# First routed mixture: six sequences are sorted inside the linear attention ahead of it, and the chunks are six and two sequences

## The reference, cut to what matters

```python
def lightning_attn(q, k, v):            # 16 heads of 64, 4 key/value heads, chunks of 128 tokens
    def step(kv, (qi, ki, vi)):
        scores = einsum('bhtd,bhsd->bhts', qi, ki) * mask
        o = einsum('bhts,bhsd->bhtd', scores, vi) + einsum('bhtd,bhde->bhte', qi * q_dec, kv)
        kv = blk_dec * kv + einsum('bhtd,bhte->bhde', ki * k_dec, vi)
        return kv, o

def mixture(x, w_gate, w1, w3, w2):      # 8 experts, the best 2 of each token, hidden width 256
    top_logits, sel = top_k(x @ w_gate, 2)
    probs = softmax(top_logits)
    y[e] = (silu(x @ w1[e]) * (x @ w3[e])) @ w2[e]
    return sum over k of probs[k] * y[sel[k]]

x = x + lightning_attention(layernorm(x))        # "light"
x = x + mixture(layernorm(x))                    # "moe1", the first one
x = x + differential_attention(layernorm(x))     # "diff"
x = x + mixture(layernorm(x))                    # "moe1", the second one
```

## Time and profile before

| what | us |
|---|---|
| median of 3 runs | 2660.44 (2657.58 to 2661.44) |
| the profiled execution | 2654.68 |
| its span | 2652.8 |
| light, first to last matmul | 1162.8 to 1546.4 |
| first mixture, light's last add to its own last add | 1547.2 to 1841.5 |
| second mixture, first to last matmul | 2367.3 to 2631.9 |

### The profile page before, as it was taken

How to read it: one execution, slowest core, us unless ns; L and a number is a source line. 1 busy time by engine, 2 the same in 40 slices (tenths; PEclk the granted TensorE clock), 3 DMA queues, 4 the chain that set the end, 5 groups by cost and what they waited for, 6 DMA issues and landing times. The chain is left out here.

```text
span 2652.8 us, 40589 instructions
## 1 busy us (share of the span) xinstructions
PE 2184.1 (82%) x11840; PEld 1313.5 (50%) x11840; DVE 1652.9 (62%) x4436; ACT 1278.5 (48%) x2252; POOL 1425.9 (54%) x1403
## 2 busy tenths in 40 slices
PE   4577997998779989989999955766999999964666
PEld 3344564666756556644444433444444444433444
DVE  6865774775667657756666644334787778744434
ACT  4643454333425443336666623433577677643333
POOL 5923654443346544436666644644767666625644
PEclk8688899999869999989999967787999999976888
DMA  1001111222011122220000032223000000021225
GB/s 49 0 3 28 38 37 50 73 96 83 1 42 37 25 78 78 96 86 1 1 1 1 1 85 58 61 83 96 1 1 1 1 0 0 1 74 54 61 68 144
DMA packets 106950, 112.45 MB, mean 42 GB/s; under 512 B 21817, under 2 KB 86201, under 8 KB 106489
## 3 DMA queue, kind: packets, MB, share of 16 engines
q1 hardware_dynamic: 97656, 91.08, 11.7%
q0 software_dynamic: 9088, 18.89, 2.1%
HBM read 71.91 MB, written 25.29 MB: 37 GB/s over the span
## 5 line engine op out<-in xcount | busy, mean ns | idle before, releaser
L2331 DVE TENSOR_REDUCE l_diffneg_max<-psum 128x1 fp32r<-128x512 f32 x512 | 335.3, 685 | 94.5 <-PE psum L2069 86.0
L2246 ACT ACTIVATE l_diffweights<-psum 128x1024 f32<-128x1024 f32 x256 | 262.0, 1026 | 128.4 <-PE psum L2098 127.4
L2069 PE MATMUL psum<-l_diffkz,l_diffQ 128*128 128x512 f32 (+1 forms) x512 | 235.4, 478 | 3.2 <-DVE l_diffneg_max L2331 2.1
L5047 POOL DMA_INDIRECT results<-l_moe1y,l_moe1xt x156 | 149.8, 961 | 157.0 <-DVE l_moe1y L4968 136.7
L2870 ACT ACTIVATE l_lightswapped<-psum 32x512 f32<-32x512 f32 x304 | 179.0, 589 | 100.8 <-DVE l_lightturned L2962 97.4
L1596 DVE TENSOR_REDUCE l_attn0neg_max<-psum 128x1 fp32r<-128x512 f32 x256 | 167.3, 683 | 53.0 <-PE psum L1330 50.3
L1502 ACT ACTIVATE l_attn0weights<-psum 128x1024 f32<-128x1024 f32 x128 | 130.2, 1023 | 121.2 <-PE psum L1352 121.1
L1723 POOL TENSOR_TENSOR l_attn0half_sums<-l_attn0weights 128x2048 f32<-128x2048 f32 x30 | 137.2, 4572 | 90.1 <-ACT l_attn0weights L1502 90.1
L4295 ACT ACTIVATE l_moe0s<-psum 128x512 f32<-128x512 f32 x144 | 85.9, 596 | 197.9 <-PE psum L855 175.1
L4715 PE MATMUL psum<-l_moe1w,l_moe1zt 128*128 x312 | 179.6, 660 | 0.0
L4731 PEld LDWEIGHTS psum<-l_moe1w,l_moe1gt 128*128 128x128 f32 x624 | 93.2, 203 | 158.1 <-issue 158.0
(11 more groups left out here) (605 smaller groups left out, 6104.2 us busy)
## 6 DMA issues: line engine op xcount, KB each, us to landing
l_moe0bcs<-gate_rows SPq DMA_DIRECT2D x64, 512.0 KB, 4.4
l_moe1xt<-sorted SPq DMA_DIRECT2D x156, 66.0 KB, 1.9
l_attn0Q<-l_attn0q_hi SPq DMA_DIRECT2D x128, 64.0 KB, 2.0
l_moe1yb<-results SPq DMA_DIRECT2D x32, 256.0 KB, 3.4
l_moe1w<-in_moe_w SPq DMA_DIRECT2D x6, 1024.0 KB, 8.3
l_attn0Q<-l_attn0q_lo SPq DMA_DIRECT2D x64, 64.0 KB, 2.0
l_moe0w_raw<-in_moe_w SPq DMA_DIRECT2D x20, 128.0 KB, 4.8
results<-l_moe1y,l_moe1xt POOLq DMA_INDIRECT x156, 2.2
```

Source lines behind the costliest of these rows:

```text
L2069: nc.tensor.matmul(ps[:, bank, :], Q[rows, n % 4, st * P:(st + 1) * P], kz[rows, n % 4, hh, :], start=True, stop=True).then_inc(pe_max.sem ...
L2246: nc.scalar.activation(weights[:, tt, 2 * pair:2 * pair + 2, :], ps[:, S[m % 2]:S[m % 2] + 2, :], ACT.Exp, scale=SCALE).then_inc(act_exp.s ...
L2331: nc.vector.tensor_reduce(neg_max[:, n % 2, st, row:row + 1], ps[:, bank_of(("max", n, b)), :], AXX, ALU.max, negate=True).then_inc(vec_ma ...
L5047: p.indirect_dma_start(core.dram["results"], bass.IndirectOffsetOnAxis(ap=xt[:, n % SLOTS, R.DEST:R.DEST + 1].bitcast(U32), axis=0), y[:, ...
```

## The change

The first mixture's preparation is cut out of routed_block into a class Sorter, with its tiles in a SortSpace that outlives a block. light_block now has a Sorter for sequences 0 to 5 (AHEAD_SEQS = 6). For sequence j it stands in three groups: in g = 2j+3 (TURNED) statistics, scale, tokens, transposes, high and low part, and gate products; in g = 2j+4 (CHOSEN) choice, ranks, weights and places; in g = 2j+5 (SORTED) the eight sorts. The transposes and ranks use bank O[1], the logits O[0]; so attend has waits that it hadn't: in chunk 3 on the low part (TURNED) or on the ranks having been read (CHOSEN). In the last group DVE makes the table; at the block's end SP writes the pads. The experts' weights (3 MB) are loaded inside light. The opening of the mixture inside light is gone, but for its gate weights, which are split in group 1.

The first mixture then has chunks of six and two sequences, 55 and 23 tiles. It starts with the tiles; sequences 6 and 7 are prepared beside the tiles of chunk 0. The six sequences of chunk 0 are read back at tiles 14 to 19 of chunk 1, one at each tile (READ = 14, step 1), and added at turns 12, 14, ... 22 (ADD = 12, BETWEEN = 2). The second mixture keeps chunks of four and four and its distances, but its Sorter does sequence 0 like all others, without the opening that diff has made for it. Statistics, scale and the split tokens have one buffer where they had two. The pads come from DRAM (16 pieces of 4224 bytes) where they came from SBUF. The second copy of the tokens is one ACT copy of 512 columns where it was four activations.

```diff
 light_block
+        def ahead(g, after):
+            j, rest = divmod(g - after - 2, KV_TILES)
+            return j if rest == 0 and 0 <= j < AHEAD_SEQS else None
+        TURNED, CHOSEN, SORTED = 1, 2, 3
 sync:
-            opening.rows_kept(sp)
+            sorter.spares(sp, spare_stored)
+            load_experts(core, sp, core.space, experts_loaded)
+            sorter.pads(sp, 0, 0)
+            for j in (AHEAD_SEQS - 2, AHEAD_SEQS - 1):
+                sorter.rows_sorted(sp, j)
+            sorter.pads_landed(sp, 0)
+            sp.wait_ge(experts_loaded, 48)
 tensor, attend(g, c):
+                if c == 3 and ahead(g, TURNED) is not None:
+                    sorter.wait(t, sorter.vec_lo, ahead(g, TURNED), "lo")
+                if c == 3 and ahead(g, CHOSEN) is not None:
+                    sorter.wait(t, sorter.chooser.vec_gate, ahead(g, CHOSEN), "ranked")
 tensor, in group g, between scores(g, 3) and attend(g, 2):
+                if ahead(g, TURNED) is not None:
+                    wait(t, act_o, g, 1)
+                    sorter.turned(t, ahead(g, TURNED), O[1])
+                if ahead(g, CHOSEN) is not None:
+                    wait(t, act_o, g, 1)
+                    sorter.ranks(t, ahead(g, CHOSEN), O[1])
 tensor, behind scores(g + 1, 0):
+                if ahead(g, TURNED) is not None:
+                    wait(t, act_o, g, 2)
+                    sorter.gate(t, ahead(g, TURNED), O[0])
 scalar, behind attended(g, 1), ahead of swap(g + 1, "q3"):
+                    sorter.tokens(a, ahead(g, TURNED))
 scalar, behind keys_turned(g + 1), ahead of attended(g, 2):
+                    sorter.high(a, ahead(g, TURNED), O[1])
 vector, in the last group, ahead of state_after(g, 2):
+                    sorter.tabled(d, 0, 0, AHEAD_SEQS * NQ * 2 + 7, AHEAD_SEQS - 1)
 routed_block
-    SEQS = (4, 4)
-    COMBINE, BETWEEN = 16, 4
+    READ, ADD, BETWEEN = (14, 12, 2) if prepared else (16, 18, 4)
+                    j, rest = divmod(t - READ, 1 if prepared else BETWEEN)
 moe1_layer
-    routed_block(core, name, store=core.last)
+    if core.sorted_ahead:
+        routed_block(core, name, core.space, (AHEAD_SEQS, NSEQ - AHEAD_SEQS), 1, False, core.last)
+    else:
+        routed_block(core, name, core.space, (4, 4), 0, True, core.last)
```

785 lines of the change are left out of this document (462 added, 323 removed).

## The result

| | before | after |
|---|---|---|
| median of the runs, us | 2660.94 (2657.58 to 2668.81, 4 runs) | 2688.11 (2685.67 to 2693.38, 4 runs) |
| profiled execution (its span) | 2654.7 (2652.8) | 2693.4 (2691.6) |

The account below looks back on a forecast made before the run. PE was taken as full in light (293 of 300 us), no engine as full in the mixture's preparation. First mixture -86, light +58, second mixture +8 make -20: profiled 2634.7 us, forecast median 2640, range 2618 to 2662.

Parts of the forecast that it names:

- Statistics, scale and shift: Light's odd groups: statistics ahead of the key's cosine make PE lose 1.5 us, the shift 0.1.
- POOL "at nothing more": Light's odd groups: POOL's 27.1 us, with eight sorts and a scale, fit in the group's 29, so cost nothing more.
- The second rival: Light: POOL's sorts are paid in series, an odd group costs 11.2 us instead of 5.2; 2676 us, chance 0.12.
- The choice, 3.3: Light's even groups: choice, marks, ranks and weights delay the keys' transposes and chunk 3's attend, 3.3 us a group.
- The third rival: Light: all sines beside sorts are slow, five a group at 0.64 us each, 19 in six groups; 2659 us, chance 0.1.
- Start of the mixture: First mixture: from light's last add to the first result 11.5 us, with SP's first transfer 1.0 behind the add.
- the fourth rival: First mixture: tiles can't start with the block because pads end behind light's last add; all ten us lost give 2650, chance 0.08.
- Chunk 1: First mixture, 23 tiles: 37 us for 22 steps plus 14 for tiles issued late behind adds, 51 in all.
- Between the chunks: First mixture: table, eight pads, their landing and the first tile take 23.4 us, and nothing of it changes.
- Second mixture: Second mixture: sequence 0's preparation now precedes the first sort, 8.7 us of which about 1 was there; 8 us longer.
- POOL's neighbourhood: Light: 3 us added because a sine product beside a POOL product took 1.33 us against a median of 0.693.
- the odd group's sum: Light, six groups with transposes and sorts: statistics, shift, tokens, low part and PE's own work, 5.2 us a group.

Follow-up runs that it names:

- e1: The kernel after, with the sorter's scale issued on POOL ahead of the group's first sort instead of behind its third: 2675.7 us.
- e2: The kernel after, with four of a sequence's eight sorts moved to the even group behind its odd one: 2707.9 us.
- e5: On top of e1, DVE's choice done in light's idle gaps, ranks read ahead of q3's sine and weights behind it: 2643.8 us.
- e11: The kernel after with e1, e5, e3 and e4 together, and the second choice's weight made from one input: 2622.5 us.
- e10: On top of e1, the choice in DVE's gaps as in e5, but ranks still read behind q3's sine: 2653.0 us.
- e3: The kernel after, with diff's eleven loads issued behind the tenth tile of the first mixture's chunk 0 instead of ahead of the first: 2686.4 us.
- e4: The kernel after, with chunk 0's results read from tile 10 and added from turn 8 in the first mixture's chunk 1: 2688.1 us.

## Why the prediction was wrong

The direction was missed through light; the mixture went nearly by its terms.

| step | forecast | measured |
|---|---|---|
| mixture: start | 11.5 | 21.4 |
| chunk 0 | 111 | 109.7 |
| between the chunks | 23.4 | 25.5 |
| chunk 1 | 51 | 52.6 |
| end | 11 | 10.3 |
| constants and memset, group 1 | 3 | 3.6 |
| a pair of groups (mean of the last five) | 8.5 | 15.5 |
| all six pairs | 51 | 88.7 |
| last group and table | 1 | 5 |
| second mixture | 8 | 12.9 (10.9 in the mean of the twelve kernels) |

- **Statistics, scale and shift** ("PE loses 1.5, and 0.1 for the shift"). This step failed. The scale's work was counted on POOL and the shift's on DVE, but not that the shift waits for the scale where POOL gets to it, although the prediction itself put three sorts and a scale in front of the values of chunk 2. The first odd stretch, without any sort, grew by 4.7, and with the scale at once by 1.7; so 3.0, and 3.8 beside sorts (e1). Statistics' 1.5 was right.
- **POOL "at nothing more"**. Right in substance once the scale is out of the way: the eight sorts cost a pair at most 2.1 (see the run with the sorts late). The second rival (sorts in series) names what the keys' transposes show, a growth above 13, but not its cause: e1 has the same sorts and gets 3.3 of the pair back, and e2 shows that fewer sorts in a group can cost more.
- **The choice, 3.3**. This step failed too, by size: it is of the right kind and too small. Its steps were priced by the mixture's rows, where POOL is idle or sorts: 0.16 to 0.19 for the difference, mark or weight. In light most of them stand beside one of POOL's products and take 0.9 to 1.03, ahead of a state, of q3's chain or of an attend. Moving them took 4.2 off a pair in all (e5: 58.2 to 54.0).
- **The third rival** was the right mechanism on the wrong instructions. The sines' mean is 0.73 in 1200 to 1500, not 1.33, with 3 of 50 over 1 us. Sorts do not hold instructions with two inputs in SBUF: the same small ones take 0.16 to 0.19 beside sorts in the mixture. It is light's own products on POOL that hold DVE, and they hold what the change adds.
- **The clock** was in no term. PE waited, its granted clock fell from 1.00 to 0.90, and its matmuls took some 40 us more. As a check: a clock 0.06 lower over 29 us cost 1.6 us in e11, and light's 482.9 us at 0.90 against 384.4 at 0.98 would by that rate make some 37 (an estimate). The edits of the scale and of the choice gave clock back (0.96, 0.99), but PE's idle time does not tell the clock: it was 33.7, 35.6 and 31.3 us in 1200 to 1500 of the kernel after, e1 and e10, at 0.90, 0.96 and 0.99. What of the waits makes it fall stays open.
- **Start of the mixture**. The wrong row was read. "SP issued its first transfer 1.0 us behind that add" is true of the earlier trace rows, but that transfer is of weights. The eleven loads for diff stood between it and the first tile before, too, hidden by 69 us of preparation. Without this cover they cost 7.6 to 8.1 (e3). SP's first load came 3.8 behind light's last add (1641.5 to 1645.3) instead of 1.0: the last pad was issued at 1641.3 and landed at 1643.4, 1.9 behind the add, and the 0.9 to SP's next load are its way out of the block, so the fourth rival happened too, at 2.8. Its 2.8 and the 7.6 on top of 11.5 make 21.9; measured were 21.4.
- **Chunk 1** was right in cause and size: 14 for the late tiles, 10 to 13 by e4. Around results 15 to 17 of it there are gaps of 6.5, 2.6 and 9.4 us where others are 1.6, fewer and larger than the four growing ones that were forecast.
- **Between the chunks**, "nothing of it changes", was wrong by 2.1 (1.4 to 2.8 in the other kernels with six sequences ahead): the pads now come from DRAM and not from SBUF. Their eight issues take 9.9 us instead of the 8.3 of the earlier trace rows, and from the first issue to the last landing it is 11.5 instead of 9.7. No run changes the pads' source alone:

```profile
1776.68 9.90 SPq L4908 DMA_DIRECT2D sorted<-pads  x8
```

- **Second mixture**. The opening's absence cost 7.6 at the first sort (18.5 less 11.0), against 8.7 less 1; the pads of its one boundary should take another 2 by the line above. The 1 to 3 left over are within the scatter of this block (298.6 to 304.9 with the same code).

Light outgrew its forecast by 40.5: 38 in the six pairs, 4 in the last group, 1.5 in the groups ahead of the first pair, less the 3 that the forecast had added for POOL's neighbourhood. Of a pair's 7.0 too much, e1 gives back 3.3 and e5 another 4.2, clock included: the two places, of the scale and of the choice, are as large as the whole error. The mixture's 11 are the eleven loads and the pads. In the odd group's sum the terms add to 5.1 and not 5.2, and 4.9 us against "some 3" is 1.9 where it counts 1.4; neither moves the forecast by more than 4.

## What to carry to other kernels

When work is moved beside other work, list for every instruction whom it waits for on another engine and what stands ahead of that one in its own queue; an engine with a third of its time free can still be late by 3.5 us for the one result that counts. A duration measured in a quiet stretch can be six times too small in a busy one (0.16 and 1.03 here): take it from a row with the same neighbours, and put the small instructions where their engine waits anyway. When preparation that hid a queue's other transfers goes, look what the queue does first, and put first what the first work needs.

## What the runs showed of the hardware

- DVE instructions of 4 to 32 elements took 0.16 to 0.19 us beside POOL's indirect DMAs. Beside its SBUF products of 1.0 to 1.27 us they took up to 1.12 in light, ending with the product, or, where a second product followed at once, with that one (2.24 and 2.45 in e2). Elsewhere in the kernel after, one of 4 elements beside a sum of 128x2048 took 4.48 of its 4.52 us. That holds for tensor_tensor and scalar_tensor_tensor with both inputs in SBUF and for most tensor_scalars and casts (a cast of 64 elements took 0.13); reciprocal (0.18), reduction (0.22), largest and index (0.15 to 0.17) were not held, nor was a tensor_tensor with one input in PSUM (0.16 to 0.19). The prediction had expected this of sines alone and feared it of sorts.
- Not every long instruction of POOL holds DVE: beside its powers of 128x4, 1.0 us each, small two-input forms took 0.15 to 0.20 us in all thirteen kernels. A few casts and tensor_scalars beside an indirect DMA took 0.28 to 0.41 and ended with it.
- PE's granted clock in 1200 to 1500 was 1.00 before (7 us idle), and 0.90, 0.96 and 0.99 with 31 to 36 us idle (after, e1, e10). With the same work and the same idle time a stretch took 27.4 at 1.00 and 29.0 at 0.94 (e11).
- A block that no edit touches took 513 to 530 us in the profiled executions, more than most edits of a few microseconds bring; only the length of the block itself told them apart.
